# New places for 76 parts in the 72-step schedule of an attention kernel

## What is computed

```python
b, s, _ = x.shape            # 2, 1024, E = 512
q = (x @ Wq)...; k = (x @ Wk)...; v = (x @ Wv)...   # 32, 8 and 8 heads
q = apply_rope(q, pos)
k = apply_rope(k, pos)
scores = jnp.einsum('bhqd,bhkd->bhqk', q, k) / jnp.sqrt(jnp.float32(D))
scores = jnp.where(causal[None, None], scores, jnp.finfo(x.dtype).min)
attn = jax.nn.softmax(scores, axis=-1)
out = jnp.einsum('bhqk,bhkd->bhqd', attn, v)
```

## Time and profile before

| | us |
|---|---|
| time, median of 3 runs (lowest, highest) | 1761.48 (1759.42, 1769.46) |
| the profiled execution's own time | 1762.95 |
| its span | 1761.2 |
| PE busy | 1693.4 (96%) |
| DVE busy | 1263.1 (72%) |
| ACT busy | 1140.9 (65%) |
| POOL busy | 985.0 (56%) |

### The profile page before, as it was taken

The page is one execution under the profiler, slowest core; times in us unless marked ns, Lnnn a source line. Parts: engine busy times, 40 slices in busy tenths (PEclk is TensorE's granted clock), DMA queues, the critical chain, the costliest instruction groups (busy, mean ns, idle before and its releaser), DMA issues. The chain is left out here.

```text
span 1761.2 us, 27586 instructions
## 1 busy us (share of the span) xinstructions
PE 1693.4 (96%) x8993; PEld 1384.4 (79%) x8993; DVE 1263.1 (72%) x2518; ACT 1140.9 (65%) x2315; POOL 985.0 (56%) x822
## 2 busy tenths in 40 slices
PE   6899999999999999999999999889999899999998
PEld 3588888888888888888888888767788688888886
DVE  6788889888888888888888888883333454535333
ACT  4588888888888888888887878873222443323222
POOL 1367767777777767776776676645100144444453
PEclk9999999999999999999999999999999899999999
DMA  7344544445445354354354444456555200101000
GB/s 289 77 107 108 137 110 121 121 112 131 108 115 134 92 133 124 102 138 111 97 138 112 107 129 119 128 152 210 170 175 169 92 1 1 55 0 54 1 31 24
DMA packets 174970, 190.92 MB, mean 108 GB/s; under 512 B 31457, under 2 KB 117737, under 8 KB 174833
## 3 DMA queue, kind: packets, MB, share of 16 engines
q1 hardware_dynamic: 137840, 140.99, 28.3%
q10 hardware_dynamic: 36992, 48.25, 9.9%
HBM read 86.12 MB, written 31.74 MB: 67 GB/s over the span
## 5 line engine op out<-in xcount | busy, mean ns | idle before, releaser
L1087 DVE TENSOR_TENSOR p_lo<-ps_b,p_hi 128x512 fp32r<-128x512 f32 x576 | 394.6, 686 | 128.9 <-ACT p_hi L972 123.9
L987 ACT ACTIVATE p<-ps_b,negm 128x640 f32<-128x640 f32 (+7 forms) x512 | 383.1, 753 | 115.9 <-DVE negm L1098 112.9
L1098 DVE CUSTOM_DVE_ANT_0 ps_b<-ps_b,mask_w 128x640 f32<-128x640 f32 (+7 forms) x512 | 382.4, 758 | 10.1 <-PE ps_b L863 8.8
L972 ACT CAST p_hi<-ps_b 128x512 fp32r<-128x512 f32 x576 | 338.7, 590 | 71.6 <-PE ps_b L874 60.5
L874 PE MATMUL ps_b<-ident,p 128*128 128x128 f32 x2304 | 351.6, 275 | 12.2 <-DVE p_lo L1087 11.5
L874 PEld LDWEIGHTS ps_b<-ident,p 128*128 128x128 f32 x2304 | 273.3, 141 | 72.3 <-DVE p_lo L1087 26.0
L862 PE MATMUL ps_b<-k_hh,q_hl 128*128 128x512 f32 (+3 forms) x768 | 265.9, 347 | 14.8 <-ACT p L987 11.1
L888 PE MATMUL ps_b<-p_hi,v_hl 128*128 128x512 f32 x576 | 262.4, 456 | 4.8 <-ACT o_sb L980 4.3
L863 PE MATMUL ps_b<-k_l,q_hl 128*128 128x512 f32 (+3 forms) x768 | 256.0, 347 | 0.0
L889 PE MATMUL ps_b<-p_lo,v_hl 128*128 128x512 f32 x576 | 227.7, 395 | 0.0
L1242 POOL TENSOR_TENSOR o_sb<-o_sb,o_low 64x512 f32<-64x512 f32 x128 | 171.8, 1347 | 65.4 <-DMA o_low<-o_sb 64.0
(11 more groups left out here) (160 smaller groups left out, 3147.0 us busy)
## 6 DMA issues: line engine op xcount, KB each, us to landing
rot_x<-rot_s SPq DMA_DIRECT2D x320, 64.0 KB, 2.0
q_hl<-rot_s SPq DMA_DIRECT2D x128, 128.0 KB, 2.5
q_hl<-rot_x SPq DMA_DIRECT2D x128, 128.0 KB, 2.7
rd_all<-reciprocals SPq DMA_DIRECT2D x128, 128.0 KB, 3.1
o_low<-o_sb ACTq DMA_DIRECT2D x128, 128.0 KB, 2.4
attention_out<-o_sb SPq DMA_DIRECT2D x128, 128.0 KB, 2.5
o_raw<-attention_out SPq DMA_DIRECT2D x32, 512.0 KB, 4.7
wf<-in_L_ffn_w_gate_up ACTq DMA_DIRECT2D x28, 256.0 KB, 3.3
```

The costliest lines, as they stand in the source:

```text
L972: act.copy(p_hi[:, T % P_RING, :], ps[:, T_BANK + T % 2, :]).then_inc(phi_ready, 1)
L987: act.activation(p_32[:, parity, h, column * P:column * P + nk], s, ACT.Exp, bias=negm[:, k:k + 1], scale=-1.0, accum_out=den[:, parity, k ...
L1087: dve.tensor_tensor(p_lo[:, T % P_RING, :], ps[:, T_BANK + T % 2, :], p_hi[:, T % P_RING, :].bitcast(F32), ALU.subtract).then_inc(plo_read ...
L1098: dve.tensor_tensor_reduce(s, s, mask_w[:, S - nk:S], 1.0, HIGHEST, ALU.add, ALU.min, negm[:, k:k + 1]).then_inc(max_ready, 1)
```

## The change

No instruction is added, removed or altered. 76 parts get another place, 30 of PE, 18 of ACT, 21 of DVE and 7 of POOL; SP's tables stay. Some entries change no order by themselves. The diff, of the tables that are followed below (cut are those of COPIES, SHIFTS, EXPONENTIALS, KEY_HIGHS, KEY_LOWS, UNIT_ABS, UNIT_DIFFERENCES, DIVISIONS and ROTARY_SUMS):

```diff
 TURNS = Places(own_tiles(0), 100, {
-    8: (7, 201), 35: (34, 511), 43: (42, 201), 71: (70, 511)})
+    2: (1, 101), 8: (7, 202), 24: (23, 101), 35: (34, 511), 43: (42, 202), 70: (69, 301), 71: (70, 511)})
...
 VALUES = Places(own_tiles(LAG), 200, {
-    0: (2, 900), 1: (4, 101), 2: (5, 101), 8: (10, 900), 9: (11, 900), 16: (18, 101), 18: (20, 900), 24: (26, 900),
-    26: (28, 511), 27: (29, 900), 32: (34, 900), 36: (38, 900), 44: (46, 501), 45: (47, 900), 52: (54, 900),
-    54: (56, 900), 55: (58, 101), 60: (62, 900), 63: (65, 900), 68: (70, 900)})
+    0: (2, 900), 1: (4, 101), 2: (5, 101), 6: (7, 203), 8: (10, 301), 9: (11, 900), 16: (19, 102), 18: (20, 900),
+    24: (26, 900), 26: (28, 511), 27: (29, 900), 32: (34, 501), 36: (38, 900), 44: (46, 501), 45: (47, 900),
+    51: (52, 301), 52: (54, 900), 54: (56, 900), 55: (58, 101), 60: (62, 900), 63: (65, 900), 68: (70, 900),
+    71: (72, 201)})
 PROJECTIONS = Places(own_pieces(), 300, {
-    (0, 0): (1, 101), (2, 0): (9, 800), (3, 0): (14, 101), (3, 1): (14, 102), (4, 0): (19, 800), (5, 0): (24, 201),
-    (5, 2): (27, 101), (6, 0): (31, 201), (7, 0): (36, 501), (7, 1): (38, 101), (9, 0): (44, 800), (10, 0): (49, 501),
-    (10, 2): (52, 101), (11, 0): (54, 800), (12, 0): (59, 501), (12, 1): (61, 201), (12, 2): (62, 101),
-    (13, 0): (67, 101)}, early=PROJECTIONS_EARLY)
+    (0, 0): (1, 103), (0, 2): (4, 102), (2, 0): (9, 800), (3, 0): (14, 101), (3, 1): (14, 102), (3, 2): (17, 101),
+    (3, 3): (17, 102), (4, 0): (19, 101), (5, 0): (24, 201), (5, 2): (27, 101), (5, 3): (27, 102), (6, 0): (29, 101),
+    (6, 1): (30, 501), (7, 0): (36, 501), (7, 1): (38, 101), (7, 2): (39, 101), (9, 0): (44, 800), (9, 1): (44, 801),
+    (10, 0): (49, 201), (10, 2): (52, 101), (11, 0): (54, 800), (12, 0): (59, 501), (12, 1): (61, 201),
+    (12, 2): (62, 101), (13, 0): (66, 102)}, early=PROJECTIONS_EARLY)
 VALUE_TURNS = Places(own_uses(("v",), 0), 400, {
     1: (6, 511), 8: (41, 201)})
 SCORES = Places(own_rows(0), 500, {
-    6: (6, 520), 14: (15, 501), 22: (24, 501), 30: (33, 520), 38: (42, 520), 46: (51, 501), 54: (60, 501), 62: (69, 520)}, early=SCORES_EARLY)
+    1: (1, 102), 3: (4, 103), 6: (7, 201), 14: (15, 501), 22: (25, 201), 29: (33, 101), 30: (33, 520), 36: (42, 201),
+    38: (42, 520), 46: (51, 501), 54: (60, 501), 58: (66, 101), 62: (69, 520)}, early=SCORES_EARLY)
 KEY_SCALES = Places({0: W_SCALE}, 100, {
-    0: (27, 201)})
+    0: (27, 601)})
...
 VALUE_HIGHS = Places(own_uses(("v",), 1), 130, {
-    8: (42, 201)})
+    1: (7, 401), 8: (42, 201)})
 HIGHS = Places(own_tiles(0), 200, {
-    11: (10, 311), 30: (29, 201), 40: (39, 601), 66: (65, 201)})
+    11: (10, 311), 12: (11, 311), 30: (29, 401), 34: (33, 301), 36: (35, 201), 40: (39, 601), 47: (46, 301),
+    54: (53, 301), 66: (65, 201)})
...
-QUERY_HIGHS = Places(own_uses(("qx", "qy"), 8), 510, early=in_warm_up(("qy",), QUERIES_AT))
...
+QUERY_HIGHS = Places(own_uses(("qx", "qy"), 8), 510, {
+    2: (17, 201)}, early=in_warm_up(("qy",), QUERIES_AT))
...
 UNIT_SIGNS = Places(own_units(3), 610, {
-    3: (43, 201)})
+    0: (5, 121), 2: (28, 201), 3: (43, 201)})
...
 MAXIMA = Places(own_rows(1), 200, {
-    3: (4, 301), 6: (7, 220), 14: (16, 220), 22: (25, 220), 25: (28, 201), 27: (31, 301), 30: (34, 220), 38: (43, 220),
-    46: (52, 220), 50: (57, 301), 54: (61, 220), 62: (70, 220)}, early=MAXIMA_EARLY)
+    3: (4, 301), 6: (7, 220), 7: (7, 221), 14: (16, 220), 17: (19, 301), 22: (25, 220), 25: (28, 204), 26: (29, 301),
+    27: (31, 301), 28: (31, 303), 30: (34, 220), 38: (43, 220), 46: (52, 220), 50: (57, 301), 54: (61, 220),
+    58: (65, 301), 62: (70, 220)}, early=MAXIMA_EARLY)
 LOWS = Places(own_tiles(0), 300, {
-    55: (55, 511)})
-RECIPROCALS = Places(own_pairs(0), 400)
+    7: (7, 201), 28: (28, 202), 55: (55, 511)})
+RECIPROCALS = Places(own_pairs(0), 400, {
+    1: (10, 301), 3: (26, 301)})
 RECIPROCAL_TURNS = Places(own_pairs(1), 410, {
-    3: (29, 701)})
+    0: (2, 301), 3: (26, 302)})
 UNIT_SUMS = Places(own_units(4), 500, {
-    0: (4, 201), 3: (41, 301)})
-UNIT_PICKS = Places(own_units(7), 510)
+    0: (4, 201), 1: (18, 101), 2: (31, 302), 3: (41, 301)})
+UNIT_PICKS = Places(own_units(7), 510, {
+    0: (9, 301), 1: (18, 401), 2: (32, 701), 5: (70, 201)})
 WEIGHT_LOWS = Places({k: W_LOW + k for k in range(CT)}, 700, {
-    2: (31, 302)})
+    0: (28, 201), 1: (28, 203), 2: (28, 205)})
 HALF_SUMS = Places(own_blocks(LAG + 3), 100, {
-    5: (29, 111), 10: (53, 401)})
...
-UNIT_HATS = Places(own_units(8), 410)
...
+UNIT_HATS = Places(own_units(8), 410, {
+    4: (53, 401)})
...
```

More of the change, by code:

```diff
@@ L451 @@
 VALUE_HIGHS = Places(own_uses(("v",), 1), 130, {
-    8: (42, 201)})
+    1: (7, 401), 8: (42, 201)})
 HIGHS = Places(own_tiles(0), 200, {
-    11: (10, 311), 30: (29, 201), 40: (39, 601), 66: (65, 201)})
+    11: (10, 311), 12: (11, 311), 30: (29, 401), 34: (33, 301), 36: (35, 201), 40: (39, 601), 47: (46, 301),
+    54: (53, 301), 66: (65, 201)})
 COPIES = Places(own_blocks(LAG), 300)
-SHIFTS = Places(own_blocks(LAG + 1), 310)
+SHIFTS = Places(own_blocks(LAG + 1), 310, {
+    4: (25, 421), 8: (45, 301)})
 EXPONENTIALS = Places(own_rows(1), 400, {
-    6: (7, 420), 14: (16, 420), 22: (25, 420), 30: (34, 420), 38: (43, 420), 46: (52, 420), 54: (61, 420), 62: (70, 420)}, early=EXPONENTIALS_EARLY)
+    6: (7, 420), 12: (15, 621), 14: (16, 420), 15: (17, 202), 22: (25, 420), 30: (34, 420), 38: (43, 420), 44: (52, 201),
+    46: (52, 420), 54: (61, 420), 62: (70, 420)}, early=EXPONENTIALS_EARLY)
 KEY_HIGHS = Places(own_uses(("kv",), 8), 500, {
-    13: (75, 601)}, early=in_warm_up(("kv",), KEYS_AT))
-QUERY_HIGHS = Places(own_uses(("qx", "qy"), 8), 510, early=in_warm_up(("qy",), QUERIES_AT))
-UNIT_ABS = Places(own_units(3), 600)
+    7: (44, 201), 13: (75, 601)}, early=in_warm_up(("kv",), KEYS_AT))
+QUERY_HIGHS = Places(own_uses(("qx", "qy"), 8), 510, {
+    2: (17, 201)}, early=in_warm_up(("qy",), QUERIES_AT))
+UNIT_ABS = Places(own_units(3), 600, {
+    1: (13, 401)})
 UNIT_SIGNS = Places(own_units(3), 610, {
-    3: (43, 201)})
+    0: (5, 121), 2: (28, 201), 3: (43, 201)})
 UNIT_STORES = Places(own_units(15), 620)
@@ L469 @@
 MAXIMA = Places(own_rows(1), 200, {
-    3: (4, 301), 6: (7, 220), 14: (16, 220), 22: (25, 220), 25: (28, 201), 27: (31, 301), 30: (34, 220), 38: (43, 220),
-    46: (52, 220), 50: (57, 301), 54: (61, 220), 62: (70, 220)}, early=MAXIMA_EARLY)
+    3: (4, 301), 6: (7, 220), 7: (7, 221), 14: (16, 220), 17: (19, 301), 22: (25, 220), 25: (28, 204), 26: (29, 301),
+    27: (31, 301), 28: (31, 303), 30: (34, 220), 38: (43, 220), 46: (52, 220), 50: (57, 301), 54: (61, 220),
+    58: (65, 301), 62: (70, 220)}, early=MAXIMA_EARLY)
 LOWS = Places(own_tiles(0), 300, {
-    55: (55, 511)})
-RECIPROCALS = Places(own_pairs(0), 400)
+    7: (7, 201), 28: (28, 202), 55: (55, 511)})
+RECIPROCALS = Places(own_pairs(0), 400, {
+    1: (10, 301), 3: (26, 301)})
 RECIPROCAL_TURNS = Places(own_pairs(1), 410, {
-    3: (29, 701)})
+    0: (2, 301), 3: (26, 302)})
 UNIT_SUMS = Places(own_units(4), 500, {
-    0: (4, 201), 3: (41, 301)})
-UNIT_PICKS = Places(own_units(7), 510)
+    0: (4, 201), 1: (18, 101), 2: (31, 302), 3: (41, 301)})
+UNIT_PICKS = Places(own_units(7), 510, {
+    0: (9, 301), 1: (18, 401), 2: (32, 701), 5: (70, 201)})
 WEIGHT_LOWS = Places({k: W_LOW + k for k in range(CT)}, 700, {
-    2: (31, 302)})
+    0: (28, 201), 1: (28, 203), 2: (28, 205)})
 HALF_SUMS = Places(own_blocks(LAG + 3), 100, {
-    5: (29, 111), 10: (53, 401)})
-DIVISIONS = Places(own_blocks(LAG + 4), 110)
+    5: (29, 111), 6: (34, 431), 10: (53, 402)})
+DIVISIONS = Places(own_blocks(LAG + 4), 110, {
+    5: (29, 112)})
 ROTARY_SUMS = Places(own_uses(("kv", "qx", "qy"), 6), 200, {
-    5: (28, 101)})
-KEY_LOWS = Places(own_uses(("kv",), 8), 300, early=in_warm_up(("kv",), KEYS_AT))
+    3: (21, 111), 5: (28, 101)})
+KEY_LOWS = Places(own_uses(("kv",), 8), 300, {
+    13: (79, 201)}, early=in_warm_up(("kv",), KEYS_AT))
 QUERY_LOWS = Places(own_uses(("qx", "qy"), 8), 310, early=in_warm_up(("qy",), QUERIES_AT))
@@ L490 @@
     5: (62, 311)})
-UNIT_HATS = Places(own_units(8), 410)
-UNIT_DIFFERENCES = Places(own_units(9), 420)
+UNIT_HATS = Places(own_units(8), 410, {
+    4: (53, 401)})
+UNIT_DIFFERENCES = Places(own_units(9), 420, {
+    1: (20, 411)})
 UNIT_MAGNITUDES = Places(own_units(10), 430)
```

## The result

The changed kernel takes 1730.79 us (median of 4 runs, 1730.66 to 1731.84), the kernel before 1762.19 us (4 runs, 1759.42 to 1769.46). The direction was right, the size was not. The profiled execution after took 1730.82 us, with a span of 1729.0.

What follows compares the result with a forecast made beforehand. PE was taken to set the pace, a group shortening only by PE's waits. Gains of 2.2 us a group, 15.4 over seven, and 0.6 in the last took 1762.95 to 1747, median forecast 1745.5; 8-in-10 range 1737 to 1758.

Steps and rivals of the forecast that it cites:

- VALUES 27: PE waits for COPIES 5 to empty the output bank; with TURNS 30, 0.71 us a group, 0.55 taken as gain.
- TURNS 57: PE waits for LOWS 55 behind UNIT_PICKS 4; 0.6 us a group, all expected to go.
- TURNS 67: PE waits for LOWS 65, 0.43 us a group; PE work put ahead was to gain 0.4.
- the six places: Six PE waits that recur in nearly every head group, 3.24 us a group in sum, 22.7 over seven groups.
- All six places clear and nothing new: Rival: the whole gain, 22.7 us and up to 2 in the last group, 1737 us; chance 0.1.
- 0.5 + 0.1 + 0.55 + 0.35 + 0.6 + 0.4 - 0.3 = 2.2: Gains expected at the six places less new waits, in us a group; 15.4 us over seven groups.
- SCORES 24: PE waits for the rotated queries' transfers, 0.38 us a group; 0.1 taken as gain.
- - 0.3: Loss in us a group allowed for new PE waits, at TURNS 31 and smaller ones.
- PROJECTIONS (2, 0): PE waits for VALUE_LOWS 1 to empty its bank, 0.62 us a group with TURNS 10; 0.5 taken as gain.
- 3w - 1.78: New wait of TURNS 31 for LOWS 29, w one WEIGHT_LOWS's length: nothing at 0.54 us, 0.38 at 0.72, 3.1 at 1.62.
- WEIGHT_LOWS held on DVE: Slower rival: POOL holds the three moved WEIGHT_LOWS to near 2.65 us, TURNS 31 waits 6.2; 1787 us; chance 0.08.
- The waits only move: Rival: DVE's full list from SCORES 24 to VALUES 31 limits PE; 0.8 us a group left, 1756 us; chance 0.2.

Runs made afterwards that it cites:

- experiment 4: Kernel before with two entries on POOL changed, UNIT_HATS 4 put ahead of HALF_SUMS 10: 1751.82 us, 0.994.
- experiment 8: Changed kernel with UNIT_HATS 4 and HALF_SUMS 10 back at their old places on POOL: 1734.06 us, 0.9843.
- experiment 10: Kernel before with six entries: new places for UNIT_PICKS 0, 1, 2 and 5, and the two entries of experiment 4: 1747.66 us, 0.9903.
- experiment 9: Changed kernel with PROJECTIONS (6, 0) and (6, 1) back at their old places: 1737.45 us, 0.9848.
- experiment 1: Kernel before with PE's 30 new places alone, the lists of ACT, DVE and POOL as before: 1793.38 us, 1.0179.
- experiment 2: Kernel before with the 46 new places of ACT, DVE and POOL, PE's list as before: 1748.92 us, 0.9919.
- experiment 6: Changed kernel with one entry undone, DIVISIONS 5 behind UNIT_SCALES 2 on POOL again: 1747.58 us, 0.9923.
- experiment 3: Kernel before with 30 entries, those around PROJECTIONS (2, 0), VALUES 27 to SCORES 28, TURNS 57 and TURNS 67: 1768.56 us, 1.0029.

## Why the prediction was right, and where it was wrong

**What bounds it: right.** PE set the pace before and after, and the gain is PE's waiting, read from starts. By starts, PE's waiting above the usual short step of each kind (of all steps of a kind, the one that a tenth lie under) was 7.2 us a group before and is 3.3 after; the other 0.1 of the 4.0 us a group are fewer changes between transposes and matmuls. The signs that I had named came true as well: UNIT_PICKS has a median of 0.68 us and no 2.8, and no step over 0.3 us is left at VALUES 27, TURNS 57 and TURNS 67.

**"The sum is ... 3.24 us a group": right as a count, wrong as a ceiling.** Counted over all seven groups the six places were 3.2 us. This is the number on which the low end of my range stood ("All six places clear and nothing new", 1737), and the kernel went below it, because the count left out every place of under some 0.3 us a group: SCORES 62 (0.24), TURNS 34 (0.21), SCORES 56 (0.12) and others.

**The sum "0.5 + 0.1 + 0.55 + 0.35 + 0.6 + 0.4 - 0.3 = 2.2": the step that failed.** The profiled execution came out 16.2 us below my 1747. Its parts:

- The six places cleared wholly. I had discounted each one, 2.5 of 3.24; they gave 3.2. That is 0.7 a group, 5 us. The largest are SCORES 24 (0.1 taken, 0.38 there) and VALUES 27 with TURNS 30 (0.55 taken, 0.80 there over all groups).
- "- 0.3" for new waits, which was the largest miss. The small waits, those gone less those new, with the fewer changes of kind, came to a gain of 0.8 a group in place of a loss of 0.3: 1.1 a group, 7.8 us. New ones are few: TURNS 2 in group 0 (1.1 us), one VALUE_TURNS 8 (0.83), and TURNS 31 (0.44) and TURNS 43 (0.43).
- The last group: 2.2 us, 0.6 taken, and part of it is the clock. The code behind it, unchanged: 2.0 us, nothing taken, and within what that part differs by from run to run.

12.8 of the 16.2 us are in groups 0 to 6 (5 + 7.8), which is 28.2 less 15.4.

**TURNS 57, the held UNIT_PICKS 4: mechanism right, size wrong.** "DVE gains up to 2.1 us and the whole 0.6 goes" held in experiment 4, which gave 1.4 us a group (10.0 over seven). I had priced the hold by the one PE wait right behind it, and the pair clears others too (TURNS 67, SCORES 24, TURNS 34); how the hold reaches those isn't shown. That it is this pair that frees UNIT_PICKS 4 in the whole change fell in experiment 8, where it is free without the pair.

**PROJECTIONS (2, 0): right, by the first of its two causes.** I gave it to UNIT_PICKS 0's move and VALUE_HIGHS 1's; experiment 10 clears it with UNIT_PICKS and the hats alone, VALUE_HIGHS 1 where it was.

**VALUES 27: right,** experiment 9. Both halves are needed: experiment 1 moved PE's without DVE's and lost 31 us. TURNS 30's wait stayed away in experiment 9 without the cover, so it isn't the projection quarters that clear it.

**TURNS 67: cleared, but not by the cover alone.** I gave it to SCORES 58 and PROJECTIONS (13, 0). The wait (0.64 to 0.66 us before, start to start, in six groups) is 0.24 to 0.31 in experiment 4, where PE's list is as before, and gone in experiment 2 too.

**TURNS 31's wait, 3w - 1.78: right in kind, 0.6 us too dear.** w came out at 0.55 and TURNS 31 doesn't wait, with a margin of 0.75 us in place of 0.13. It waits in one group of seven, the one where WEIGHT_LOWS 2 took 1.69 us behind a rotary sum whose start depends on a transfer: 0.44 us, where the formula gives 1.02 (0.56 + 0.55 + 1.69 - 1.78). I had missed that DVE stood idle for 0.24 us ahead of LOWS 29, and that DVE's next instruction starts 0.09 us before the drawn end of each WEIGHT_LOWS.

**The slower rival, "WEIGHT_LOWS held on DVE": not what happened, but one entry away.** Its size was well guessed (2.65 us; 2.60 measured), its place was not: it strikes WEIGHT_LOWS 3 and PROJECTIONS (6, 3), not the three moved ones and TURNS 31. What prevents it is the entry DIVISIONS 5: (29, 112), for which the prediction had no sentence, and it is the costliest single entry that was tried (0.9923 less 0.9821, experiment 6). Of the groups' gain of 28.2 us, 13.9 would not be there without it. I had looked at what POOL does at the new place of the moved instructions, and not at what the shifted times do to those that stay.

**"The waits only move": wrong.** Between SCORES 24 and VALUES 31 DVE was full, and it still is (13.43 of 13.80 us), while PE's waits there are gone: the full list was no wall. Part of what filled it had been holds (0.94 and 0.95 us for the first two WEIGHT_LOWS of group 3, now 0.55).

Open: why SCORES 24's and TURNS 67's waits go with UNIT_HATS 4; and how the gain divides among the entries not tried apart, since the halves of experiments 1 and 2 don't add up.

## What to carry to other kernels

When work is moved in in-order lists, look at every pair of DVE and POOL instructions that come to lie side by side, the unmoved ones too: a DVE instruction with two SBUF inputs cost up to 2 us more where POOL instructions ran beside it, and one place more or less on POOL's list decided 1.0% here. Read both "busy" rows with that in mind: 14 us of PE's busy time and 25 us in the durations of two of DVE's lines were waiting, seen only in starts and in the spread of durations of one line. A wait can also cost more than itself, when the clock falls behind it (experiments 1 and 3). And don't take the sum of the places that stand out as the most that a rearrangement can give, nor cost coupled lists one by one.
